# Third graph layer: the transposes of the next group's gathered rows move from the end of the second half step to right behind its first-weight matmuls

## What the reference computes

```
e_feat = concat([x[src], x[dst], edge_attr_32])      # per edge, 96 features
h      = relu(e_feat @ W1 + b1)                      # 64 hidden
v      = h @ W2 + b2                                 # 32
x_cand = segment_max(v, dst)                         # per node
x      = layernorm(x + maximum(x_cand, x))
```

## Time and profile before

| | us |
|---|---|
| median of 3 runs | 20,992.71 |
| lowest and highest run | 20,983.97 and 21,042.5 |
| profiled execution | 21,020.92 |
| its span, first to last instruction | 21,018.7 |

### The profile page before, as it was taken

One profiled execution on the slowest core, in us unless ns is written; L12 is line 12 of the kernel. 1 busy time (PEld: TensorE's weight loads), 2 busy tenths in 40 slices (PEclk: granted clock), 3 DMA queues, 4 the chain that ended last, 5 costly groups with the idle time before them and its releaser, 6 DMA issues. The chain is left out here.

```text
span 21018.7 us, 295438 instructions
## 1 busy us (share of the span) xinstructions
PE 13077.6 (62%) x92471; PEld 7366.7 (35%) x92471; DVE 11200.6 (53%) x19689; ACT 3071.4 (15%) x5120; POOL 11786.1 (56%) x10055
## 2 busy tenths in 40 slices
PE   0565555555554776676767652555555555699999
PEld 0344434333333444444444431212222112355554
DVE  2565544444444777777777773333322222567777
ACT  0222222222221111111111110111111111000000
POOL 4788888888885555555555554666666655100000
PEclk6565555555556888888888876666666666899999
DMA  7333333333333222222222213333333333489998
GB/s 276 47 40 37 37 38 39 38 37 37 38 38 46 48 48 46 47 48 46 47 45 48 46 40 34 71 72 70 73 71 71 70 71 69 128 258 291 290 292 266
DMA packets 3008049, 1817.19 MB, mean 86 GB/s; under 512 B 1739874, under 2 KB 2765227, under 8 KB 2988427
## 3 DMA queue, kind: packets, MB, share of 16 engines
q1 hardware_dynamic: 2211164, 1336.91, 24.3%
q0 software_dynamic: 669312, 166.80, 10.8%
q10 hardware_dynamic: 126512, 300.38, 4.1%
HBM read 1474.43 MB, written 392.90 MB: 89 GB/s over the span
## 5 line engine op out<-in xcount | busy, mean ns | idle before, releaser
L2005 POOL DMA_INDIRECT xg<-d_tab,s_i x3136 | 3256.6, 1038 | 2638.1 <-POOLq L1996 1646.2
L2545 POOL DMA_INDIRECT xg<-d_tab,s_i x3136 | 3001.6, 957 | 1901.5 <-POOLq L2541 951.9
L2265 PE MATMUL pR<-w,H 128*128 128x384 f32 x6272 | 2711.8, 562 | 1426.1 <-PEq L2259 799.8
L1403 POOL DMA_INDIRECT d_acc<-AG,ix x1568 | 2466.8, 1573 | 527.3 <-issue 458.7
L1403 POOL DMA_INDIRECT d_acc<-T,ix x1568 | 2467.2, 1573 | 478.1 <-issue 442.1
L2933 PE MATMUL pacc<-nodes,HB 128*32 128x512 fp8e4 x47040 | 2662.3, 380 | 48.9 <-PEq L2977 48.9
L2582 DVE TENSOR_TENSOR_SCAN U<-mU,U,up 128x512 f32<-128x512 f32 x392 | 501.6, 1279 | 3332.9 <-DVEq L2581 2748.1
L2265 PEld LDWEIGHTS pR<-w,H 128*128 128x128 f32 x6272 | 1231.3, 216 | 2554.7 <-issue 2204.3
L2705 PE MATMUL hb<-U,Wbc 128*128 128x512 f32 x784 | 645.5, 919 | 2217.8 <-PEq L2699 2047.3
L1756 PE MATMUL pm<-ms,eq 128*128 128x32 f32 x6272 | 1365.8, 399 | 888.4 <-PEq L1754 886.2
L2933 PEld LDWEIGHTS pacc<-nodes,HB 128*32 128x32 f16 x47040 | 1260.5, 97 | 1323.7 <-issue 62.9
(11 more groups left out here) (338 smaller groups left out, 17497.6 us busy)
## 6 DMA issues: line engine op xcount, KB each, us to landing
packed<-d_A SPq DMA_DIRECT2D x420, 1792.0 KB
row<-d_m SPq DMA_DIRECT2D x1568, 64.0 KB
xg<-d_tab,s_i POOLq DMA_INDIRECT x6272
wrow<-d_w SPq DMA_DIRECT2D x196, 512.0 KB
d_scan<-so ACTq DMA_DIRECT2D x392, 256.0 KB
d_A<-stage ACTq DMA_DIRECT2D x97, 784.0 KB, 3.3
d_ea<-in_ea_t ACTq DMA_DIRECT2D x1, 50176.0 KB
d_exp<-T ACTq DMA_DIRECT2D x1, 50176.0 KB, 250.8
```

Source lines behind the costliest of these rows:

```text
L1403: e.indirect_dma_start(out=d_acc[i], out_offset=bass.IndirectOffsetOnAxis(ap=ix[k][:, t:t + 1], axis=0), in_=mo[k][:, t * F:(t + 1) * F], ...
L2005: e.indirect_dma_start(out=xg[k][:, t, :], out_offset=None, in_=d_tab, in_offset=bass.IndirectOffsetOnAxis(ap=s_i[n][:, t:t + 1], axis=0)) ...
L2265: last = e.matmul(pR[u % 2][:, j, 0:384], H[k][:, (2 * u + j) * P:(2 * u + j + 1) * P], w2[:, :], start=True, stop=True)
L2545: e.indirect_dma_start(out=xg[n][:, j * ST + c, :], out_offset=None, in_=d_tab, in_offset=bass.IndirectOffsetOnAxis(ap=s_i[d][:, col:col + ...
```

## The change

In the second half step of every group PE's call of `features` for the next group stands behind the two products into hb and ahead of `turn`; before, it stood behind everything else of that half step, in the main loop behind the count's matmuls as well. The count of landed gathers that it waits for is handed to `step`.

```diff
-                    def step(r, q, first=False, last=False):
+                    def step(r, q, first=False, last=False, count=None):
...
                         e.matmul(hb[q][:, :], Wa[64 * q:64 * (q + 1), :], XT[64 * q:64 * (q + 1), :], start=False, stop=True
                                  ).then_inc(S("hz"), 1)
+                        if count is not None:
+                            features((r + 1) % 8, count)
                         if not last:
                             turn(r if q == 0 else (r + 1) % 8, 1 - q)
...
                         for i in range(16):
-                            step((i // 2 + 2) % 8, i % 2)
+                            step((i // 2 + 2) % 8, i % 2,
+                                 count=(c - MID) * 512 + ((i // 2 + 3) // 4 + 1) * 256 if i % 2 else None)
                             for w in range(2 * i - 2, 2 * i + 2 if i == 15 else 2 * i):
                                 if w >= 0:
                                     count_sums(e, A, n, w)
-                            if i % 2:
-                                features((i // 2 + 3) % 8, (c - MID) * 512 + ((i // 2 + 3) // 4 + 1) * 256)
...
-                    step(0, 1, first=True)
-                    features(1, 256)
+                    step(0, 1, first=True, count=256)
...
-                    step(2, 1)
-                    features(3, G // 4 * 256)
+                    step(2, 1, count=G // 4 * 256)
```

More of the change, by code:

```diff
@@ L2726, in _ @@
                     step(0, 0, first=True)
-                    step(0, 1, first=True)
-                    features(1, 256)
+                    step(0, 1, first=True, count=256)
                     step(1, 0)
-                    step(1, 1)
-                    features(2, 256)
+                    step(1, 1, count=256)
                     over_chunks(e, LATE, chunk)
                     step(2, 0)
-                    step(2, 1)
-                    features(3, G // 4 * 256)
+                    step(2, 1, count=G // 4 * 256)
                     step(3, 0)
```

## The result

The changed kernel takes 21,463.91 us (median of 4 runs, 21,412.1 to 21,481.02), the kernel before in the same comparison 20,999.72 us (4 runs): a ratio of 1.0209, 95% interval 1.0193 to 1.0225, or 464 us more. The profiled execution took 21,470.34 us, with a span of 21,468.2 us and a mean granted clock of 0.725 (before 0.731). Slower was forecast, but by 149 us, and the time lies above the range.

The account below looks back on a forecast made before the run. The third layer's edge stage was taken as bound by gathers, late release of PE's signals and a tail. +96 us for U last, +77 for pairs, −24 for their groups gave +149 on 20,993: 21,142 us, range 20,840 to 21,320.

Parts of the forecast that it names:

- a cycle of gathers, release and tail: Third layer's edge stage: 20 us of gathers, 3 us until PE's signals arrive, then the way to GpSimd's restart.
- the late end: Signal of the up transposes after the change: arrives with the last signals, 13.64 us behind the relu, not at 4.40.
- the release: About 3 us after a batch's last gather, when all of PE's outstanding signals were said to arrive together.
- the first stretch: Earlier trace, XT early at 15,246.72: next batch follows gapless, next group stalls, two groups take 54.66 us against 51.45.
- Theory A: Experiments' theory: gathers hold PE's signals from some 9 us in until 3 us after; early buffer returns make costly gapless pairs.
- The price of a pair: Two groups in the edge stage, the next batch started early and gapless: +3.21 us, for 24 pairs +77 us.
- The bound of all pairs: Upper end of the unknown in the edge stage: all pairs of groups losing 3.21 us, +313 us.
- The term of +0.49 us for U as the new tail: First-half matmuls wait last for U, not XT: +0.49 us a group, 195 groups, +96 us.
- It cancels: Rival, edge stage: some groups start a microsecond or so sooner, paying for the others' 0.49 us; 20,930 to 21,056 us, chance 0.26.
- Both signals beat the stall: Rival, edge stage: xp and up come out before the hold; 20,890 us, at the extreme about 20,000 us; chance 0.18.
- A constant lag: Rival: XT follows PE's reported transposes by a fixed 11 us, steps shorten by 2.5 us; about 20,500 us, chance 0.06.
- two stretches: Places in the earlier trace where XT already came early: one pair of groups cost +3.21 us, the other −1.06 us.

Follow-up runs that it names:

- experiment 1: The changed kernel with the gather buffer given back by completion of the first first-half matmul, not by PE's sequencer: 20,968.67 us, 0.9942 of the kernel before.
- experiment 7: The changed kernel without SyncE's loads of ef in the loop, first contents used on: 21,239.03 us in a single run, 1.019 of the kernel before.
- experiments 5: The changed kernel with the gather buffer given back by the third up transpose of the first half step: 20,997.72 us, 1.0082 of the kernel before.
- experiment 10: The changed kernel with GpSimd waiting for its batch's landing, then filling a scratch tile twice, behind each batch: 20,927.97 us, 0.9935 of the kernel before.
- experiment 12: The kernel before with GpSimd waiting for its batch's landing, then filling a scratch tile twice, behind each batch: 20,870.28 us, 0.9962 of the kernel before.

## Why the prediction was right in sign and wrong in size

**Right:** XT starts early, 1.05 us behind the relu's start in the pair's held group (15,031.55 − 15,030.50 of the same timeline) and not 13.64. PE then waits for U. GpSimd's time splits into gapless batches and long waits, 1,328.4 us in 93. All of it is in the stage. With half the gathers the step of the kernel before falls by the batch, as a cycle of gathers, release and tail should.

**The step that failed** is "I take the late end for most groups, since the release is what sets the last signal, and the first stretch for one group in eight". Up is not held to the release: in the groups shown U starts 0.88 us behind XT (15,032.43) and 1.36 us behind it (15,045.27), both with no release to wait for. It is not always free either. Over the 87 groups whose return started a gapless batch, U starts 4.1 us behind XT in the median and over 3 us in 50, and the group is ready 13.6 us into the running batch in the median, so many get out after the 9 us that the prediction and Theory A gave as the start of the stall. That is early enough all the same: nearly every second group gives its buffer back while a batch still runs, 85 pairs and not 24. The price of a pair was also too small, 5.27 us and not 3.21. Part of that is its base: the two groups of 51.45 us that it was measured against hold a wait for a new list, and against 2 × 25.13 us the same stretch costs 4.40 us. And in that stretch GpSimd waited 11.28 us; the changed kernel's pairs make it wait 15.6 us. In the stretch shown above both halves of the held group still had to run after the release. The bound of all pairs, +313 us, was therefore no bound. The term of +0.49 us for U as the new tail had hardly a group left to apply to, and does not show in those: the 19 single steps are 24.69 us in the median, those of before 24.67 us (173).

**The rivals.** *It cancels* did not come about. *Both signals beat the stall* was right about the signals in most groups and wrong about the time: a group that escapes, in 12.36 us, starts the next batch too early for the group behind it. The prediction had this against it from two stretches, and gave it too few groups. *A constant lag* is out: XT follows a group's xp by 1.24 us (15,031.55 − 15,030.31) and not by 11.

The rule of the Trainium skill that the prediction set aside (page "Perfetto Trace Analysis", section "Tensor Engine Instruction (MATMUL, LD_WEIGHTS)": the reported start is real, the signal lies outside the window) agrees with experiment 1 in that the signal comes apart from the work. There relu and U start 0.09 us apart at the release (14,721.82 and 14,721.91), though PE does the transposes up, 0.66 us, between the two signals: the work was done before, and the signals were late. How exact the reported starts are, no run shows.

**Open:** by what the gathers hold back PE's signals. The loads of ef by SyncE are excluded as the cause of the pairs (experiment 7); no run shows the mechanism. Why the return by the transposes up brought 76 gapless gaps and the one by the first matmul 31 (experiments 5 and 1) is not shown either.

## What to carry to other kernels

Where one engine's long batch holds back another's signals, a signal brought forward past the hold also brings forward the start of the next batch, and that one may hit work which ran free before: follow two rounds, not one. Look for stretches of the trace of before in which the new order already happens by chance, and take their share as the unknown that it is. When rounds begin to alternate between short and long, a small fixed pause or a later return of the buffer is worth a run; but look who waits then, since a pause can make the paused engine the one that sets the round.

## What the hardware showed unexpectedly

- A running batch of 16 indirect gathers on GpSimd (20 us) holds back most of what waits on PE's results until 3.1 to 4.1 us behind its last gather (3.07 us in the earlier trace rows, 4.1 in the changed kernel's timeline). In experiment 1 the signal of xp still passes 6.3 us into the batch (XT at 14,705.10), that of matmuls reported 11.6 us into it (14,710.40) does not. Where the batch follows another without a gap the hold goes through: in the changed kernel matmuls reported 1.2 us into it (15,000.99) have their reader at 15,024.67. The hold is not a full stop. For the second half step before, PE reports xp, up, pb and pw by 14,989.8, and their readers start one at a time: XT at 14,990.07, U at 14,997.29, the copy of pb at 15,006.56, a store of pw at 15,021.22, while the gathers run or just behind them. SyncE's four loads of ef take 12.61 us to issue in it and 2.19 us outside it (at 15,027.25 after the change).
- The clock goes along with the rhythm. In the held group the matmuls hb take 2.04 us, in the group that escapes 1.10 us, the durations at the lower and the higher of TensorE's two clock levels (1.2 and 2.4 GHz). Of 86 gapless batches, 75 were started by the group right behind one whose hb matmuls all ran at the higher level; of the 105 others, 9. Which of the two drives the other no run shows. The granted clock over the stage is 0.66, before 0.68.
- The level by itself cost little where GpSimd sets the round. In experiment 10 the hb matmuls run wholly at the higher level in 193 of 196 groups, in experiment 12 in 1 of 196 (granted clock 0.71 and 0.66, 13,100 to 17,600 us), and the steps are 24.55 and 24.65 us.
